# A decoder layer's self-attention prologue: token split moved from slot 12 to slot 7, norms one slot sooner, a transpose to the end of its slot

## The reference, cut to what matters

```python
q = (hidden_states @ Wq.T).reshape(b, t, HEADS, FEAT).transpose(0, 2, 1, 3)
k = (hidden_states @ Wk.T).reshape(b, t, HEADS, FEAT).transpose(0, 2, 1, 3)
v = (hidden_states @ Wv.T).reshape(b, t, HEADS, HD).transpose(0, 2, 1, 3)
phi_q = _feature_map(q, gamma, beta)   # (x - mean) / sqrt(var + eps) * gamma + beta over 16 features,
phi_k = _feature_map(k, gamma, beta)   # then all products of two of them
kv_cum = jnp.cumsum(phi_k[..., :, None] * v[..., None, :], axis=2)
num = jnp.einsum('bhtf,bhtfd->bhtd', phi_q, kv_cum)
den = jnp.einsum('bhtf,bhtf->bht', phi_q, jnp.cumsum(phi_k, axis=2))[..., None] + EPS
y = (num / den).transpose(0, 2, 1, 3).reshape(b, t, HEADS * HD)
x = _layernorm(x + y @ Wo.T)
```

## Time and profile before

| | us |
|---|---|
| median of 3 runs | 1288.47 (1286.87 to 1291.5) |
| the profiled execution | 1291.7 |
| its span | 1290.0 |
| PE busy in the span | 1172.4 (91%) |
| DVE busy | 725.9 (56%) |
| ACT busy | 592.1 (46%) |
| POOL busy | 715.3 (55%) |

### The profile page before, as it was taken

How to read it: one execution, slowest core, us unless ns; L and a number is a source line. 1 busy time by engine, 2 the same in 40 slices (tenths; PEclk the granted TensorE clock), 3 DMA queues, 4 the chain that set the end, 5 groups by cost and what they waited for, 6 DMA issues and landing times.

```text
span 1290.0 us, 18849 instructions
## 1 busy us (share of the span) xinstructions
PE 1172.4 (91%) x6456; PEld 685.7 (53%) x6456; DVE 725.9 (56%) x1297; ACT 592.1 (46%) x1031; POOL 715.3 (55%) x617
## 2 busy tenths in 40 slices
PE   3789797879999999999999999999999999999991
PEld 2456464545555555555555555555554466566661
DVE  7686867662466744657835556835665654423222
ACT  5676767624445643545543545444443423222222
POOL 2284656325587775678785776875766132422222
PEclk9899999979999999999999999999998999999996
DMA  6009700001000000100000100000003742332324
GB/s 200 17 9 337 254 2 1 1 1 26 1 1 1 26 1 2 42 1 1 26 34 1 43 1 26 9 26 17 1 1 130 262 103 43 74 45 46 47 37 143
DMA packets 38926, 65.75 MB, mean 51 GB/s; under 512 B 4129, under 2 KB 31393, under 8 KB 38561
## 3 DMA queue, kind: packets, MB, share of 16 engines
q1 hardware_dynamic: 25792, 49.45, 12.0%
q0 software_dynamic: 7152, 9.38, 4.4%
q10 hardware_dynamic: 5888, 5.72, 1.7%
HBM read 50.96 MB, written 30.61 MB: 63 GB/s over the span
## 4 chain that ended last, share of the span: by engine, by line
PE 74%; DVE 15%; issue 4%; ACT 4%; DMA 2%; ACTq 1%; another core or an unknown queue 0%; POOL 0%; SPq 0%; DVEq 0%; POOLq 0%
PE PS L1896 16%; PE PS L1907 12%; PE PS L1783 10%; PE PS L1973 9%; DVE mxp L1511 5%; PE PS L1991 5%; PE PS L1802 3%; PE PS L227 3%; PE PS L1694 2%; PE PS L1704 2%; PE PS L228 2%; PE PS L229 2%; PE PS L1683 2%; PE PS L1982 1%; PE PS L1877 1%
## 5 line engine op out<-in xcount | busy, mean ns | idle before, releaser
L732 POOL TENSOR_TENSOR acc<-acc,PX 128x1024 f32<-128x1024 f32 (+1 forms) x165 | 392.9, 2381 | 127.5 <-ACT PX L1012 118.8
L1012 ACT ACTIVATE PX<-PS 128x1024 f32<-128x1024 f32 (+1 forms) x208 | 212.5, 1026 | 261.9 <-PE PS L1896 256.3
L1511 DVE TENSOR_REDUCE mxp<-PS 128x2 f32<-128x804 f32 x256 | 243.1, 990 | 127.1 <-PE PS L1802 126.2
L1907 PE MATMUL PS<-PX,V 128*64 128x512 f32 (+1 forms) x832 | 209.4, 613 | 0.2 <-ACT PX L1012 0.2
L787 POOL DMA_INDIRECT Y<-yb,goal_u x39 | 60.8, 1558 | 183.6 <-DVE yb L1600 144.2
L1973 PE MATMUL PS<-W,XBT 128*128 x312 | 147.1, 594 | 1.6 <-issue 0.8
L664 POOL TENSOR_SCALAR_AFFINE_SELECT A<-A 128x128 f32<-128x128 f32 x256 | 85.4, 350 | 111.2 <-ACT A L899 108.3
L899 ACT ACTIVATE A<-PS 128x512 f32<-128x512 f32 (+3 forms) x256 | 97.7, 445 | 65.0 <-PE PS L1694 63.8
L1896 PE MATMUL PS<-QH,KH 64*128 64x512 f32 (+1 forms) x416 | 102.3, 488 | 4.8 <-ACT PX L1012 3.2
L1896 PEld LDWEIGHTS PS<-QH,KH 64*128 64x128 f32 (+1 forms) x416 | 38.1, 179 | 117.9 <-issue 81.3
L1907 PEld LDWEIGHTS PS<-PX,V 128*64 128x64 f32 (+1 forms) x832 | 48.6, 137 | 79.1 <-issue 73.2
(11 more groups left out here) (293 smaller groups left out, 2105.5 us busy)
## 6 DMA issues: line engine op xcount, KB each, us to landing
W<-in_w SPq DMA_DIRECT2D x24, 512.0 KB, 4.8
XB<-XG ACTq DMA_DIRECT2D x39, 130.0 KB, 2.1
X<-in_x SPq DMA_DIRECT2D x1, 2048.0 KB, 12.0
Y<-X SPq DMA_DIRECT2D x4, 512.0 KB, 3.4
X<-Y SPq DMA_DIRECT2D x4, 512.0 KB, 5.5
out<-X SPq DMA_DIRECT2D x8, 256.0 KB, 2.1
xt_raw<-in_xt SPq DMA_DIRECT2D x3, 512.0 KB, 3.9
c_raw<-in_ctxt SPq DMA_DIRECT2D x6, 200.0 KB, 2.7
```

The lines of the kernel that those rows point to most:

```text
L732: ins = pool.tensor_tensor(sums[0:r], sums[0:r], PX[0:r, (NL * p + t) % NP, :, :], ALU.add)
L1012: act.activation(PX[0:r, u % NP, :, :], PS[0:r, score_buffer(u):score_buffer(u) + 2, :], ACT.Exp, scale=XD ** -0.5)\
L1511: dve.tensor_reduce(mxp[:, p % 2, :, v % NT, v // NT:v // NT + 1].rearrange("p a o -> p (a o)"), PS[:, k:k + 2, 0:BW], AX, ALU.max)\
L1907: mm = pe.matmul(PS[rows, 4, :], V[0:LROWS[j], j, P * p + XD * half:P * p + XD * half + XD], PX[0:LROWS[j], u % NP, half, :], start=(j == ...
```

## The change

Three lines. The square root, the normalisation and the affine of each token tile are listed one slot sooner, so the square root is in the same slot as the variance it needs. The token split ("x") of the batch after the next is listed in slot 7, where it was in slot 12. In slot 12 none of TensorE's steps is issued among the scores; its one step there, the first "yt", is issued behind the values, in all four batches.

```diff
--- before.py
+++ after.py
@@ -474,7 +474,7 @@
                      13: [("vs", 1), ("turn q", 0, 0), ("turn k", 0, 0)], 14: [("vs", 2), ("turn q", 0, 1), ("turn k", 0, 1)],
                      15: [("turn q", 1, 0), ("turn k", 1, 0)]}
             for i in range(NT):
-                for after, kind in ((0, "project qk"), (1, "square"), (2, "variance"), (3, "deviation"), (4, "normalise"), (5, "affine")):
+                for after, kind in ((0, "project qk"), (1, "square"), (2, "variance"), (2, "deviation"), (3, "normalise"), (4, "affine")):
                     ahead.setdefault(2 * i + after, []).insert(0, (kind, i))
                 ahead.setdefault((1, 2, 5, 6)[i], []).append(("project v", i))
                 ahead.setdefault((1, 2, 5, 6)[i], []).append(("vcopy", i))
@@ -483,7 +483,7 @@
                     own.setdefault((1, 2, 4, 5)[k], []).append(("weights low", k))
             return ([(-1, s) for s in rest.get(n, []) if not first] + [(0, s) for s in own.get(n, [])]
                     + ([(1, s) for s in ahead.get(n, [])] if more else [])
-                    + ([(2, ("x",))] if n == 12 and b + 2 < B else []))
+                    + ([(2, ("x",))] if n == 7 and b + 2 < B else []))
 
         SCORE_BANKS = (3, 4, 5)
 
@@ -1753,7 +1753,7 @@
             def attention(b, more):
                 for n in range(SLOTS):
                     steps = [(d, s) for d, s in alongside(n, b) if s[0] in PE_STEPS]
-                    half = (len(steps) + 1) // 2
+                    half = 0 if n == 12 else (len(steps) + 1) // 2
                     others = [s for s in meanwhile(n, b) if s[0] != "ctx"]
                     for j in range(4):
                         if n + 1 < SLOTS:
```

## The result

| | before | after |
|---|---|---|
| median of four runs each, us | 1288.69 (1286.87 to 1291.5) | 1311.76 (1308.49 to 1313.55) |
| the profiled execution, us | 1291.7 | 1310.56 |
| its span, us | 1290.0 | 1308.8 |
| mean granted clock of the span | 0.97 | 0.955 |
| PE, DVE, ACT, POOL busy, us | 1172.4, 725.9, 592.1, 715.3 | 1185.5, 731.3, 593.6, 708.2 |

The change makes the kernel slower: the ratio is 1.0178, interval 1.0152 to 1.0204, 23.1 us. I had forecast 1296.0, slower by 7.5, in a range that ended at 1301. The direction was right, but what came is three times that size.

What follows compares the result with a forecast made beforehand. VectorE's unbroken run in slots 7 to 12 was taken to bound self-attention batches. Batches 0 to 3 gave +2.5, +2.3, +0.8 and +1.9, together +7.5 us on the 1288.47 median: 1296.0, range 1287 to 1301.

Steps and rivals of the forecast that it cites:

- Late start, tile 0: Slots 3 and 4: normalise ahead of VectorE's other steps delays TensorE, 1.35 us in batch 0, 1.95 in batches 1 and 2.
- rival (c): Longer waits in slots 4, 8, 9 put 1.2 GHz stretches into slots 13 to 15: +12 us, 1300.5; chance 0.12.
- Its parts added up give 18.4: VectorE's run, slot 7's copy to the last split: 18.4 us without token split, against 19.6 before; batch 2 1.2 shorter.
- The wait in slot 9 at nothing: TensorE stops some 3 us behind tile 3's square root, but VectorE's run goes on beneath: nothing added to the sum.
- Token split, 1.2 and 1.1 per batch: Slot 7, batches 0 and 1: subtraction adds 1.22 us to VectorE's run, blocking by GpSimd 1.1 more (bounds 0 and 1.27).
- the 0.9 forecast for ScalarE's copy: Token copy ahead of "turn q" in slot 7 lengthens TensorE's slot 8 wait by 0.9 us, covered by VectorE's run.
- Batch 3, +1.9: Slot 12 of batch 3: moved transposes make the row maxima start 1.9 us later; bounds 0 and 1.9.
- y_l's wait of over 4 us: Sign that the forecast is right: in batch 3 VectorE's y_l waits over 4 us, where it waited 2.39 before.
- Waits removed: TensorE's waits for masks (slot 10, 1.86 us) and y (slot 12, 1.48) go; gain counted 0.5 batch 0, 0.7 batch 1.
- (a): Waits in slots 10 and 12 and lower-clock stretches simply go: 11.2 us faster, 1277.3; chance 0.15.
- (b): Removed waits in slots 10 and 12 pay for late start and batch 3, GpSimd meetings dissolving: +2, 1290.5; chance 0.13.

Runs made afterwards that it cites:

- the change with dummies: The whole change plus unread TensorE transposes filling its waits in slots 4 and 9 and, in batch 3, 11 and 12; ratio 1.0114 to the kernel before.
- the norms of tiles 2 and 3: Kernel before with only tiles 2 and 3 normed one slot sooner, the affine of tile 3 left in slot 11; ratio 1.0020 to the kernel before.
- the affine of tile 3 late: Kernel before with only the norms one slot sooner, but GpSimd's affine of tile 3 left in slot 11; ratio 1.0083 to the kernel before.
- The late square root: Kernel before with only the norms one slot sooner, but the square root of tile 3 left in slot 9; ratio 1.0100 to the kernel before.
- the move and dummies alone: Kernel before with only the slot 12 transposes moved, plus unread TensorE transposes in batch 3's waits of slots 11 and 12; ratio 1.0000 to the kernel before.

## Why the prediction was wrong, point by point

- **Late start, tile 0** (+1.35, +1.95, +1.95): right. It is 1.9 us in batch 2, and 1.4 and 1.9 in batches 0 and 1 where no stretch at 1.2 GHz fell into it (the change with dummies).
- **The clock, rival (c), chance 0.12:** this is the first step that failed. The sum had the clock at nothing; it stood beside the sum, in slots 13 to 15 and at 4.5 us. By the dummies it is 8.3 us of 23.1, and by the time at 1.2 GHz that was left with them that isn't all. It cost where TensorE is dense behind a wait: slots 4 to 7, and slots 12 to 15 in batch 3. The stretch in slot 0 of batch 1 has no longer wait ahead of it that the trace shows. In slots 13 to 15 of the other batches a cost is not excluded; one execution of the norms of tiles 2 and 3 has such a stretch there, in a batch 1 of 60.8 instead of 58.1 us.
- **"Its parts added up give 18.4":** the second step that failed. The run of batch 2 grew by 1.4 us instead of shrinking by 1.2, and the three runs grew by 5.7 for 1.5. Adding VectorE's instructions took for granted that its idle time would vanish; 0.2 to 0.4 us stayed at the copy of slot 11 and 0.6 to 1.6 at the last split. And the affine of tile 2, which the sum had meeting nothing, met the layer norm, for 0.9 to 1.1 us. The affine of tile 3 did meet two adjacent splits, 1.76 and 1.68 us, as the sum had it; but I asked only that, and not what is queued behind it on GpSimd. With that affine behind the masks 0.8 to 2.6 us per batch come back, by the masks or by those splits. (The working is a little off too: 19.6 less the 1.03 us of idle time is 18.6.)
- **The wait in slot 9 at nothing:** it came, 3.49 us in batch 1, 3.3 in batch 2 and none over 0.4 in batch 0. No cost of it shows: with the affine of tile 3 late it stands there at 3.33 us and the run is that of before. The late square root is no test of this, since the wait moved to slot 11.
- **Token split, 1.2 and 1.1 per batch:** the 1.2 was right, the 1.1 was not. The instruction was not blocked, the layer norm behind it was, by 0.9; and with the norms moved and no tokens it is blocked too, by 1.1. TensorE's wait in slot 8 grew from 1.21 to 1.95 us, close to the 0.9 forecast for ScalarE's copy. The Trainium skill's page "SBUF — State Buffer", section "Who interferes with whom", says that whoever issues first blocks the other; the trace agrees, with GpSimd's 2.26 us behind a VectorE instruction issued 90 ns earlier. Which of the two comes first was the guess; my bounds of 0 and 1.27 held it, my pick did not.
- **Batch 3, +1.9:** y_l's wait of over 4 us was right at full clock (4.29). The cost was 0 with the move and dummies alone (79.2 us), 3.4 in the whole change with dummies (82.8, with 24 us at 1.2 GHz), and 5.3 to 6.9 without dummies.
- **Waits removed** in slots 10 and 12: gone, as forecast, but in batch 0 the wait for masks came back in slot 11. The wait in slot 12 was worth nothing by itself (1.0008), where the sum had 0.5 and 0.7 us; that in slot 10 was never taken away alone.
- **Rivals (a) and (b):** out. Nothing got faster, and nothing evened out.

The range ended at 1301 because rival (c) was priced at three stretches of 1.5 us on top of my sum. The 14.8 us that stay with the dummies would have passed it by themselves.

## What to carry to other kernels

A step moved forward in one engine's list is paid by what stands behind it in every in-order queue that it passes: ask this for each engine, the one that only masks included. When you add up an engine's work, keep its idle time in until something shows that it goes. In this kernel a wait on TensorE could have a second price, the clock of what follows: 1.3 to 1.6 us per stretch where dense products followed, and nothing that could be seen where TensorE would wait again. Dummy products in the wait, with the wait itself left in place, tell the two apart, if the kernel before gets them too. Before counting on the end of a wait, check that the engine isn't merely early there: the wait for y gave nothing back when it went, and the one in slot 9 only moved.

## What the runs showed that I had not expected

A layer norm of four instructions on 128x256 values, each with one SBUF tensor and two columns of scalars as operands, was held up beside GpSimd's affine as the splits, with two tensors, were: 1.39, 2.50 and 3.35 us with none, one and both instructions beside it. And the time at 1.2 GHz in one batch is not the same from kernel to kernel even where the list is: batch 3 has the same steps in the kernel before and in the one that moves the transposes in batches 0 to 2 alone, and 20.5 us at 1.2 GHz in each, but the first has a stretch from 223.9 us and the second one from 262.8 instead. So one profile shows what such a stretch costs, not how often it comes; for that I went by the ratio of many runs.
